# A causal attention kernel: the scores of the fifth row tile split as 256 and 384 keys instead of 512 and 128

## The chip, the cores and the metric

The kernel runs on one core of a Trainium2 chip, in one launch. The metric is the device time of that launch in microseconds (us); less is better. The core has five engines that run side by side and meet at semaphores: TensorE (PE in the profile; its weight loads are shown apart as PEld), VectorE (DVE), ScalarE (ACT), GpSimd (POOL) and SyncE (SP), which issues the loads and stores here.

## The reference

It is a layer norm followed by attention and a feed-forward part, both added to the input. What matters for the change is the attention, causal, with 16 heads of 128 columns over 2 batches of 1024 rows:

```python
q = (x @ Wq + bq).reshape(b, h, t, dh)
k = (x @ Wk + bk).reshape(b, t, h, dh).transpose(0, 2, 3, 1)
v = (x @ Wv + bv).reshape(b, t, h, dh).transpose(0, 2, 1, 3)
logits = jnp.einsum('bhtd,bhds->bhts', q, k) * scale
mask = jnp.triu(jnp.full((t, t), -jnp.inf, dtype=x.dtype), k=1)
weights = jax.nn.softmax(logits + mask, axis=-1)
out = jnp.einsum('bhts,bhsd->bhtd', weights, v)
```

All of it is float32. The input has 2048 rows of 256 columns, so there are 32 pairs of batch and head; they are called heads 0 to 31 here.

## The kernel before, in words

**Split products.** Each float32 operand is held as a high and a low part, and every product is three matmuls (`split_matmul`, lines 39 to 43): high by high (L41), high by low (L42), low by high (L43). So each operand that TensorE makes must come out of PSUM twice: ScalarE writes the high part, VectorE then subtracts it and writes the low part.

**Stages.** The norm, the first Q projections and the feed-forward part take the time up to about 324 us. Then come 256 steps, 8 for each head, one for each row tile of 128 rows (`for s in range(NH * TILES)`). Tile i needs the scores of (i + 1) * 128 keys. In a step TensorE transposes the probabilities of three steps ago (L1117), makes the scores of the present tile into one of two pairs of PSUM banks, and does a piece of other work: a projection of K or V, an output product, or a product of probabilities with V. The scores go to VectorE (mask and maximum, L921), to ScalarE (exponential, L480), to GpSimd (reciprocal and scaling, L696 and L699), and come back as transposes. The transposed blocks leave PSUM by ScalarE (`pt_hi`, L466) and VectorE (`pt_lo`, L832).

**Jobs and their one bank.** Projections of K and V and output products are called jobs. The tables `EVEN` and `ODD` put them into the steps, as FIRST (ahead of the scores), EARLY (behind them) or LATE. Nearly all share one PSUM bank, `M`. Before a job starts, TensorE waits (`run`, `freed_by`) until the low part of the job before it in that bank has been written by VectorE, as that is its last reader. In step 1 of a head the job K1 makes the right half of that head's keys (512 of them); the next job in `M` comes behind the scores of step 2, and is the output product O0a in even heads and the V projection V3 in odd ones. Some heads differ: heads 0 and 1 have no job in step 2, and in heads 7, 15 and 23 (`new_group`) steps 1, 2, 4 and 5 also hold Q projections of the next group. The K1 of head 31 is run in step 5 of head 30, with the output product O1a behind it in step 6.

**K buffers.** The left half of K lies in `k_even` or `k_odd`, by the head's number, each 512 columns wide; the right half in `k_right`. The fifth tile (i = QT = 4) needs 640 keys, and its scores are two groups of three matmuls: 512 keys of the left buffer into the first bank, 128 keys of the right buffer into the second.

**What sets the order.** Each engine's order is written out in the program; none is planned at run time. On ScalarE and VectorE a FIRST job is taken out of PSUM in step 1 ahead of what the step goes on with: on VectorE the masked maximum and the `pt_lo` of the next step stand behind it.

Of the kernel before, what the change touches and what calls it, by code (L numbers as in the profile page):

```python
# [12 lines left out]
F32, F32R = mybir.dt.float32, mybir.dt.float32r  # L13
BF16, I32, F8 = mybir.dt.bfloat16, mybir.dt.int32, mybir.dt.float8e4
ACT = mybir.ActivationFunctionType
ALU = mybir.AluOpType
AX = mybir.AxisListType

P = 128
BATCH, SEQ, DM = 2, 1024, 256  # L20
TOK = BATCH * SEQ
HEADS, DH = 16, 128
# [4 lines left out]
N = 512  # L27
# [7 lines left out]
def flat(ap):  # L35
    return ap.rearrange("p a b -> p (a b)")


def split_matmul(nc, out, w_hi, w_lo, m_hi, m_lo, start, stop):

    nc.tensor.matmul(out, w_hi, m_hi, start=start, stop=False)  # L41
    nc.tensor.matmul(out, w_hi, m_lo, start=False, stop=False)  # L42
    return nc.tensor.matmul(out, w_lo, m_hi, start=False, stop=stop)  # L43
# [12 lines left out]
def attention(nc, sh, d, out):  # L56
# [7 lines left out]
    QT = N // P  # L64
# [10 lines left out]
    S = [ps[:, 0:2, :], ps[:, 2:4, :]]  # L75
# [5 lines left out]
    with ExitStack() as c:  # L81
        sb = lambda name, shape, dt: c.enter_context(nc.sbuf_tensor(name, shape, dt))
        sem = lambda name: c.enter_context(nc.semaphore(name))
        minus_one = sh["minus_one"]
        mask_row = sb("mask_row", [P, SEQ], BF16)
        bq, bk, bv, wq_in, kv_in, kv_hi, kv_lo = (
            sh[name] for name in ("bq", "bk", "bv", "wq_in", "kv_in", "kv_hi", "kv_lo"))
# [4 lines left out]
        wq_hi, wq_lo = sb("wq_hi", [P, LOADS, KC, DH], F32R), sb("wq_lo", [P, LOADS, KC, DH], F32R)  # L92
        q_all = sb("q_all", [P, GROUP, SEQ // HEADS, HEADS], F32)
        q_hi, q_lo = sb("q_hi", [P, 2, N], F32R), sb("q_lo", [P, 2, N], F32R)
        k_even = [sb(name, [P, N], F32R) for name in ("k_hi_even", "k_lo_even")]
        neg_max, row_sum, inv_sum = (sb(name, [P, 2 * TILES], F32) for name in ("neg_max", "row_sum", "inv_sum"))


# [12 lines left out]
            minus_half, var_eps, rstd = (eb(name, [P, NT], F32) for name in ("minus_half", "var_eps", "rstd"))  # L111
        pt_hi, pt_lo = (sb(name, [P, 42, P], F32R) for name in ("pt_hi", "pt_lo"))
        o_hi, o_lo = sb("o_hi", [P, N], F32R), sb("o_lo", [P, N], F32R)
        k_odd = [sb(name, [P, N], F32R) for name in ("k_hi_odd", "k_lo_odd")]
        k_right = [sb(name, [P, N], F32R) for name in ("k_hi_right", "k_lo_right")]
        probs_all = sb("probs", [P, 26 * P], F32)
        v_hi, v_lo = (sb(name, [P, 2, TILES, DH], F32R) for name in ("v_hi", "v_lo"))
# [60 lines left out]
        def job_of(h, i, where):  # L178

            name = JOBS[h].get(i, {}).get(where)  # L180
            if name is None:
                return None
            if name[0] == "K":
                return ("K", h if name == "K1" else h + 1, int(name[1]))
            if name[0] == "V":
                return ("V", h // 2, int(name[1]))
            return ("O", h - 1, int(name[1]), "ab".index(name[2]))
# [15 lines left out]
        probs = lambda s, i: probs_all[:, (0, 5, 11, 18)[i % 4] * P:((0, 5, 11, 18)[i % 4] + i + 1) * P]  # L203
# [4 lines left out]
        def k_of(h, half):  # L208

            if half and h + 1 == NH:  # L210
                return [t[:, 0:N] for t in wq_space]
            return [t[:] for t in (k_right if half else (k_even, k_odd)[h % 2])]

        def q_of(h, half):

# [26 lines left out]
        bank_of = lambda *turn: S[place[turn] % 2]  # L242
# [25 lines left out]
        bank_for = lambda job: elsewhere.get(job, M)  # L268
# [112 lines left out]
        def _(act):  # L381
# [56 lines left out]
            def evacuate(job):  # L438

                if job is None or job[0] == "O":  # L440
                    return
                act.wait_ge(job_done, nth[job])
                if job[0] == "K":
                    _, h, half = job
                    ins = nc.scalar.activation(k_of(h, half)[0], bank_for(job), ACT.Identity,
                                               bias=bk[:, h % HEADS:h % HEADS + 1])
                else:
                    ins = nc.scalar.activation(v_view(v_hi, job[2]), as_v(bank_for(job)), ACT.Copy)  # L448
                ins.then_inc(job_hi_done, 1)
# [90 lines left out]
            for s in range(NH * TILES):  # L540
                h, i = divmod(s, TILES)
# [173 lines left out]
        def _(dve):  # L715
# [64 lines left out]
            def evacuate(job):  # L780

                if job is None:
                    return
                if job[0] == "K":
                    _, h, half = job
                    dve.wait_ge(job_hi_done, nth_hi[job])
                    k_hi, k_lo = k_of(h, half)
                    ins = nc.vector.scalar_tensor_tensor(k_lo, bank_for(job), bk[:, h % HEADS:h % HEADS + 1],
                                                         k_hi.bitcast(F32), ALU.add, ALU.subtract)
                elif job[0] == "V":  # L790
                    dve.wait_ge(job_hi_done, nth_hi[job])
                    ins = nc.vector.tensor_tensor(v_view(v_lo, job[2]), as_v(bank_for(job)),  # L792
                                                  v_view(v_hi, job[2]).bitcast(F32), ALU.subtract)
                else:
                    _, h, half, ab = job
                    dve.wait_ge(job_done, nth[job])
                    g = h // HEADS * (SEQ // P // 2) + 2 * half + ab
                    sums = flat_acc[:, g * PAIR:(g + 1) * PAIR]
                    ins = nc.vector.tensor_tensor(sums, bank_for(job), sums, ALU.add)  # L799
                ins.then_inc(job_lo_done, 1)  # L800

            def wq_low(n):
                dve.wait_ge(wq_hi_done, n + 1)
                slot = n % LOADS
                nc.vector.tensor_tensor(  # L805
                    flat(wq_lo[:, slot, :, :]), flat(wq_in[:, slot, :, :]), flat(wq_hi[:, slot, :, :]).bitcast(F32),
                    ALU.subtract).then_inc(wq_lo_done, 1)
# [18 lines left out]
            def pt_low(s, ch):  # L826

                i = tile_at(s)
                at = chunk_no(s, ch)
                blocks = min(QT, i + 1 - ch * QT)  # L830
                dve.wait_ge(pt_hi_done, at + 1)
                nc.vector.tensor_tensor(  # L832
                    pt_blocks(pt_lo, i, ch), T[at % 2][:, 0:blocks * P].rearrange("p (a b) -> p a b", b=P),
                    pt_blocks(pt_hi, i, ch).bitcast(F32), ALU.subtract).then_inc(pt_lo_done, 1)
# [76 lines left out]
            for s in range(NH * TILES):  # L911
                h, i = divmod(s, TILES)
                if s:
                    evacuate(job_of(*divmod(s - 1, TILES), LATE))
                if s >= LAG:
                    for ch in range(banks_of(tile_at(s - LAG))):
                        pt_low(s - LAG, ch)
                evacuate(job_of(h, i, FIRST))
                dve.wait_ge(scores_done, s + 1)
                tile, width = tile_of(h, i), (tile_of(h, i) + 1) * P  # L920
                nc.vector.tensor_tensor_reduce(  # L921
                    probs(s, tile), flat(bank_of("S", h, tile))[:, 0:width], mask_row[:, SEQ - width:SEQ],
                    -1.0, -MASKED, ALU.add, ALU.min, neg_max[:, s % 16:s % 16 + 1]).then_inc(max_done, 1)
                evacuate(job_of(h, i, EARLY))
                if s == 1:
                    add_down(*halves_at(STEPS + 1))
                    add_down(*halves_at(STEPS + 2))
                for m in o_after(h, i):
                    o_low(h - 1, m)
                if i < 2 and new_group(h):  # L930
                    for n in (2 * i, 2 * i + 1):
                        wq_low((h + 1) // GROUP * HEADS + n)
                for u in q_steps(h, i):
                    q_step(h // GROUP + 1, u)
# [15 lines left out]
        def _(pe):  # L950
# [135 lines left out]
            def scores(s):  # L1086
                h, i = divmod(s, TILES)
                tile = tile_of(h, i)
                bank_free("S", h, tile)
                if i == 0:  # L1090
                    pe.wait_ge(job_lo_done, nth[("K", h, 0)])
                if tile == QT:
                    pe.wait_ge(job_lo_done, nth[("K", h, 1)])
                half, cols = tile // QT, slice(tile % QT * P, (tile % QT + 1) * P)
                if i == 0 or tile == QT:
                    pe.wait_ge(q_lo_done, 2 * h + half + 1)
                hi, lo = q_of(h, half)
                for bank in range(half + 1):
                    width = min(N, (tile + 1) * P - bank * N)
                    keys_hi, keys_lo = k_of(h, bank)  # L1100
                    last = split_matmul(nc, bank_of("S", h, tile)[:, bank, 0:width], hi[:, cols], lo[:, cols],
                                        keys_hi[:, 0:width], keys_lo[:, 0:width], True, True)
                last.then_inc(scores_done, 1)

# [60 lines left out]
            for k in range(STEPS):  # L1165
# [9 lines left out]
                if k == BO_ROW_AT:  # L1175
                    pe.wait_ge(bo_wide_done, KC)
                    pe.wait_ge(wt_lo_done, 2 + k // 4)
                    for h in range(KC):
                        last = nc.tensor.transpose(M[:, h * P:(h + 1) * P], bo_wide[:, h, :], ident[:])
# [5 lines left out]
            for s in range(NH * TILES):  # L1185
                h, i = divmod(s, TILES)
# [73 lines left out]
```

## Time and profile before

| | us |
|---|---|
| median of 3 runs | 1260.76 (1258.79 to 1262.61) |
| the profiled execution's own time | 1260.4 |
| its span, first to last instruction | 1258.6 |
| PE busy / PEld busy | 1225.3 / 1084.6 |
| DVE / ACT / POOL busy | 876.2 / 741.1 / 742.7 |

The mean granted TensorE clock is 0.992 of full. In the timeline an instruction has its start and duration. Matmuls are pipelined and overlap in it, so that what one costs is the distance from its start to the start of the next one, not its duration; a weight load (PEld) normally starts when the matmul ahead of the one that it serves starts. Short waits of TensorE are not marked in brackets: they are seen as a weight load that starts late.

### The profile page before, as it was taken

What the parts mean: (1) busy time and instruction counts of PE and PEld (TensorE: products, weight loads), DVE (VectorE), ACT (ScalarE), POOL (GpSimd) and SP (SyncE); (2) the same over time, 40 slices, a digit from 0 to 9 for tenths busy, and PEclk for the clock granted to TensorE, in tenths of its full rate; (3) what the DMA queues carried; (4) which work ended last, traced back from release to release, by engine and by line L of the source; (5) the groups of instructions that cost most, each with busy time, mean ns of one, the idle gap of its engine ahead of it and who ended that gap; (6) DMA issues with size and microseconds to landing.
All of it is one profiled execution on the core that took longest, in us unless ns stands there. A gap on an engine that the chain in (4) does not pass through costs nothing.

```text
span 1258.6 us, 20567 instructions
## 1 busy us (share of the span) xinstructions
PE 1225.3 (97%) x7556; PEld 1084.6 (86%) x7556; DVE 876.2 (70%) x1695; ACT 741.1 (59%) x1534; POOL 742.7 (59%) x784
## 2 busy tenths in 40 slices
PE   8999999999999999999999999999999999999997
PEld 7788888888889999779999888899899779899886
DVE  8877777776766676656777666667677666676664
ACT  4544444444676667556676665576667566666653
POOL 6445545553676667347676742676767337677753
PEclk9999999999999999999999999999999999999999
DMA  6100000000000000110000011010000200000001
GB/s 151 46 7 14 13 14 11 23 1 9 13 13 14 27 14 13 51 30 27 13 14 14 25 36 47 14 46 14 26 14 13 64 1 22 18 14 14 14 5 34
DMA packets 57331, 29.87 MB, mean 24 GB/s; under 512 B 16272, under 2 KB 57232, under 8 KB 57232
## 3 DMA queue, kind: packets, MB, share of 16 engines
q1 hardware_dynamic: 56016, 27.62, 7.9%
q8 instruction: 62, 1.02, 0.3%
q10 hardware_dynamic: 1216, 0.93, 0.2%
q14 instruction: 37, 0.30, 0.1%
HBM read 26.44 MB, written 2.10 MB: 23 GB/s over the span
## 4 chain that ended last, share of the span: by engine, by line
PE 88%; DVE 7%; ACT 3%; POOL 1%; issue 1%; DMA 0%; ACTq 0%; POOLq 0%
PE ps L41 26%; PE ps L43 26%; PE ps L42 26%; PE ps L1117 9%; ACT probs L480 1%; DVE pt_lo L832 1%; DVE xn_rows L736 1%; DVE probs L921 1%; PE ps L985 1%; DVE wq_lo L805 1%; DVE q_all L814 1%; POOL probs L699 1%; ACT pt_hi L466 1%; DVE stats L721 0%; ACT wq_hi L386 0%
## 5 line engine op out<-in xcount | busy, mean ns | idle before, releaser
L699 POOL TENSOR_TENSOR probs<-probs,inv_sum 128x128 f32<-128x128 f32 (+7 forms) x256 | 294.9, 1152 | 20.0
L696 POOL TENSOR_TENSOR inv_sum<-row_sum,minus_one 128x1 f32<-128x1 f32 x256 | 141.1, 551 | 258.2 <-ACT probs L480 257.1
L480 ACT ACTIVATE probs<-probs,neg_max 128x128 f32<-128x128 f32 (+7 forms) x256 | 198.8, 777 | 109.6 <-DVE neg_max L921 107.1
L466 ACT ACTIVATE pt_hi<-ps 128x512 fp32r<-128x512 f32 (+3 forms) x384 | 173.7, 488 | 92.1 <-PE ps L1117 89.1
L832 DVE TENSOR_TENSOR pt_lo<-ps,pt_hi 128x512 fp32r<-128x512 f32 (+3 forms) x384 | 200.8, 551 | 16.9 <-ACT pt_hi L466 16.7
L921 DVE CUSTOM_DVE_ANT_0 probs<-ps,mask_row 128x128 f32<-128x128 f32 (+7 forms) x256 | 192.0, 750 | 14.7 <-PE ps L43 8.2
L1117 PE MATMUL ps<-ident,probs 128*128 128x128 f32 x1152 | 169.6, 275 | 5.2 <-DVE pt_lo L832 3.9
L682 POOL TENSOR_TENSOR hid_lo<-act_buf,hid_hi 128x512 fp32r<-128x512 f32 x64 | 82.9, 1295 | 140.7 <-ACT hid_hi L420 140.7
L1117 PEld LDWEIGHTS ps<-ident,probs 128*128 128x128 f32 x1152 | 134.9, 142 | 18.7 <-issue 8.9
L42 PE MATMUL ps<-pt_lo,v_hi 128*128 128x512 f32 (+3 forms) x386 | 133.8, 347 | 0.0
L43 PE MATMUL ps<-pt_hi,v_lo 128*128 128x512 f32 (+3 forms) x386 | 133.5, 346 | 0.0
L41 PE MATMUL ps<-pt_hi,v_hi 128*128 128x512 f32 (+3 forms) x386 | 131.2, 340 | 0.0
L799 DVE TENSOR_TENSOR acc<-ps,acc 128x512 f32<-128x512 f32 x128 | 87.6, 685 | 58.9 <-PE ps L43 58.8
L589 POOL TENSOR_TENSOR q_lo<-q_all,q_hi 128x512 fp32r<-128x512 f32 x63 | 81.8, 1299 | 71.3 <-ACT q_hi L457 71.3
L515 ACT ACTIVATE act_buf<-ps 128x512 f32<-128x512 f32 x64 | 38.3, 599 | 132.7 <-PE ps L43 132.7
L840 DVE SCALAR_TENSOR_TENSOR o_lo<-ps,bv,o_hi 128x512 fp32r<-128x512 f32 x63 | 47.3, 751 | 81.0 <-ACT o_hi L473 81.0
L41 PE MATMUL ps<-xn_hi,w_hi 128*128 128x512 f32 x256 | 102.9, 402 | 0.7 <-DVE act_buf L891 0.5
L42 PE MATMUL ps<-xn_lo,w_hi 128*128 128x512 f32 x256 | 101.3, 396 | 0.0
L43 PE MATMUL ps<-xn_hi,w_lo 128*128 128x512 f32 x256 | 101.0, 395 | 0.0
L792 DVE TENSOR_TENSOR v_lo<-ps,v_hi 128x512 fp32r<-128x512 f32 x64 | 44.3, 692 | 59.4 <-ACT v_hi L448 59.4
L41 PEld LDWEIGHTS ps<-pt_hi,v_hi 128*128 128x128 f32 x386 | 73.5, 190 | 9.0
L42 PEld LDWEIGHTS ps<-pt_lo,v_hi 128*128 128x128 f32 x386 | 73.2, 190 | 9.0
(151 smaller groups left out, 3394.4 us busy)
## 6 DMA issues: line engine op xcount, KB each, us to landing
wq_in<-in_wq SPq DMA_DIRECT2D x63, 128.0 KB, 2.3
kv_in<-in_wk SPq DMA_DIRECT2D x16, 256.0 KB, 2.5
wo_in<-in_wo SPq DMA_DIRECT2D x32, 128.0 KB, 2.0
kv_in<-in_wv SPq DMA_DIRECT2D x32, 128.0 KB, 2.3
out<-acc SPq DMA_DIRECT2D x8, 256.0 KB, 2.4
acc<-in_x SPq DMA_DIRECT2D x2, 512.0 KB, 5.5
raw<-in_gate SPq DMA_DIRECT2D x16, 64.0 KB, 1.7
raw<-in_up SPq DMA_DIRECT2D x16, 64.0 KB, 2.1
```

What stands on the lines that cost most here:

```text
L41: nc.tensor.matmul(out, w_hi, m_hi, start=start, stop=False)
L42: nc.tensor.matmul(out, w_hi, m_lo, start=False, stop=False)
L43: return nc.tensor.matmul(out, w_lo, m_hi, start=False, stop=stop)
L466: nc.scalar.activation(pt_blocks(pt_hi, i, ch), T[at % 2][:, 0:blocks * P].rearrange("p (a b) -> p a b", b=P), ACT.Copy).then_inc(pt_hi_do ...
L480: nc.scalar.activation(row, row, ACT.Exp, bias=neg_max[:, s % 16:s % 16 + 1], scale=-1.0, accum_out=row_sum[:, s % 16:s % 16 + 1]).then_in ...
L682: nc.gpsimd.tensor_tensor(hid_lo[:, k % 4, :], act_buf[:, k % 4, :], hid_hi[:, k % 4, :].bitcast(F32), ALU.subtract).then_inc(hid_lo_done, 1)
L696: nc.gpsimd.tensor_tensor(inv_sum[:, at], row_sum[:, at], minus_one[:], ALU.pow).then_inc(inv_done, 1)
L699: nc.gpsimd.tensor_tensor(row, row, inv_sum[:, at].to_broadcast([P, (tile_of(h, i) + 1) * P]), ALU.mult).then_inc(probs_done, 1)
L799: ins = nc.vector.tensor_tensor(sums, bank_for(job), sums, ALU.add)
L832: nc.vector.tensor_tensor(pt_blocks(pt_lo, i, ch), T[at % 2][:, 0:blocks * P].rearrange("p (a b) -> p a b", b=P), pt_blocks(pt_hi, i, ch). ...
L921: nc.vector.tensor_tensor_reduce(probs(s, tile), flat(bank_of("S", h, tile))[:, 0:width], mask_row[:, SEQ - width:SEQ], -1.0, -MASKED, ALU ...
L1117: last = nc.tensor.transpose(T[at % 2][:, n * P:(n + 1) * P], probs(s, i)[:, b * P:(b + 1) * P], ident[:])
```

## The change

The left K buffers become 640 columns wide. When the right half of K leaves PSUM, its first 128 keys are also written into the new fifth block of the left buffer, by an extra instruction on ScalarE and one on VectorE, each ahead of the one that writes the 512 columns. The fifth tile's scores are then 256 keys and 384 keys, all from the left buffer. They lie in columns 256 to 895 of the two banks, next to one another as before, and VectorE reads them from there.

```diff
-        k_even = [sb(name, [P, N], F32R) for name in ("k_hi_even", "k_lo_even")]
+        k_even = [sb(name, [P, N + P], F32R) for name in ("k_hi_even", "k_lo_even")]
-        k_odd = [sb(name, [P, N], F32R) for name in ("k_hi_odd", "k_lo_odd")]
+        k_odd = [sb(name, [P, N + P], F32R) for name in ("k_hi_odd", "k_lo_odd")]
...
+        k_fifth = lambda h: [t[:, N:N + P] for t in (k_even, k_odd)[h % 2]]
+        k_middle = lambda h: [t[:, 2 * P:N + P] for t in (k_even, k_odd)[h % 2]]
+        score_cols = lambda tile: slice(2 * P, 2 * P + N + P) if tile == QT else slice(0, (tile + 1) * P)
...
                 act.wait_ge(job_done, nth[job])
                 if job[0] == "K":
                     _, h, half = job
+                    if half:
+                        nc.scalar.activation(k_fifth(h)[0], bank_for(job)[:, 0:P], ACT.Identity,
+                                             bias=bk[:, h % HEADS:h % HEADS + 1])
                     ins = nc.scalar.activation(k_of(h, half)[0], bank_for(job), ACT.Identity,
                                                bias=bk[:, h % HEADS:h % HEADS + 1])
...
                     dve.wait_ge(job_hi_done, nth_hi[job])
+                    if half:
+                        k_hi, k_lo = k_fifth(h)
+                        nc.vector.scalar_tensor_tensor(k_lo, bank_for(job)[:, 0:P], bk[:, h % HEADS:h % HEADS + 1],
+                                                       k_hi.bitcast(F32), ALU.add, ALU.subtract)
                     k_hi, k_lo = k_of(h, half)
                     ins = nc.vector.scalar_tensor_tensor(k_lo, bank_for(job), bk[:, h % HEADS:h % HEADS + 1],
                                                          k_hi.bitcast(F32), ALU.add, ALU.subtract)
...
-                    probs(s, tile), flat(bank_of("S", h, tile))[:, 0:width], mask_row[:, SEQ - width:SEQ],
+                    probs(s, tile), flat(bank_of("S", h, tile))[:, score_cols(tile)], mask_row[:, SEQ - width:SEQ],
...
-                    width = min(N, (tile + 1) * P - bank * N)
+                    first, width = 0, min(N, (tile + 1) * P - bank * N)
                     keys_hi, keys_lo = k_of(h, bank)
-                    last = split_matmul(nc, bank_of("S", h, tile)[:, bank, 0:width], hi[:, cols], lo[:, cols],
+                    if tile == QT and bank == 0:
+                        first, width = 2 * P, 2 * P
+                    elif tile == QT:
+                        width = 3 * P
+                        keys_hi, keys_lo = k_middle(h)
+                    last = split_matmul(nc, bank_of("S", h, tile)[:, bank, first:first + width], hi[:, cols], lo[:, cols],
```

On VectorE, step 1 and the start of step 2 and 3 of an even head read before as follows (`k_lo_right` is the low part of the right half, L921 the masked maximum of scores, `acc` takes up the output product O0a):

```order
L832 TENSOR_TENSOR pt_lo<-ps,pt_hi 128x3x128 [waits pt_hi_done]
L788 SCALAR_TENSOR_TENSOR k_lo_right<-ps,bk,k_hi_right 128x512 [waits job_hi_done]
L921 ISA probs,neg_max<-ps,mask_row 128x256 [waits scores_done]
L921 ISA neg_max 128x1
L832 TENSOR_TENSOR pt_lo<-ps,pt_hi 128x4x128 [waits pt_hi_done] x2
L921 ISA probs,neg_max<-ps,mask_row 128x384 [waits scores_done]
L921 ISA neg_max 128x1
L799 TENSOR_TENSOR acc<-ps,acc 128x512 [waits job_done]
```

The same place now, in the changed kernel's line numbers:

```order
L843 TENSOR_TENSOR pt_lo<-ps,pt_hi 128x3x128 [waits pt_hi_done]
L796 SCALAR_TENSOR_TENSOR k_lo_even<-ps,bk,k_hi_even 128x128 [waits job_hi_done]
L799 SCALAR_TENSOR_TENSOR k_lo_right<-ps,bk,k_hi_right 128x512
L932 ISA probs,neg_max<-ps,mask_row 128x256 [waits scores_done]
L932 ISA neg_max 128x1
L843 TENSOR_TENSOR pt_lo<-ps,pt_hi 128x4x128 [waits pt_hi_done] x2
L932 ISA probs,neg_max<-ps,mask_row 128x384 [waits scores_done]
L932 ISA neg_max 128x1
L810 TENSOR_TENSOR acc<-ps,acc 128x512 [waits job_done]
```

One instruction of 128 columns is new, and the wait for ScalarE's high parts moved to it; all else of the step stands behind both. ScalarE has the like: the 128-column write (L450) first, with the wait for the job, then the 512-column one (L452).

On TensorE, the fifth tile of an even head read before (`k_hi_even` is the left buffer, `k_hi_right` the right one, `vw_hi` the start of the V projection behind it):

```order
L1117 MATMUL ps<-ident,probs 128x128
L41 MATMUL ps<-k_hi_even,q_hi 128x512 [waits q_lo_done,job_lo_done,max_done]
L42 MATMUL ps<-k_lo_even,q_hi 128x512
L43 MATMUL ps<-k_hi_even,q_lo 128x512
L41 MATMUL ps<-k_hi_right,q_hi 128x128
L42 MATMUL ps<-k_lo_right,q_hi 128x128
L43 MATMUL ps<-k_hi_right,q_lo 128x128
L41 MATMUL ps<-vw_hi,xn_hi 128x256 [waits vw_lo_done,job_lo_done]
```

And now:

```order
L1133 MATMUL ps<-ident,probs 128x128
L41 MATMUL ps<-k_hi_even,q_hi 128x256 [waits q_lo_done,job_lo_done,max_done]
L42 MATMUL ps<-k_lo_even,q_hi 128x256
L43 MATMUL ps<-k_hi_even,q_lo 128x256
L41 MATMUL ps<-k_hi_even,q_hi 128x384
L42 MATMUL ps<-k_lo_even,q_hi 128x384
L43 MATMUL ps<-k_hi_even,q_lo 128x384
L41 MATMUL ps<-vw_hi,xn_hi 128x256 [waits vw_lo_done,job_lo_done]
```

The count of matmuls and the sum of their columns stay; only the widths and the buffer of the second three differ.

## Rows read from the trace of the kernel before

**Rows 1.** The page, chain that ended last, share of the span by engine
```profile
PE 88%; DVE 7%; ACT 3%; POOL 1%; issue 1%; DMA 0%; ACTq 0%; POOLq 0%
```

**Rows 2.** Timeline of PE, fifth tile of head 14: start, duration, instruction
```profile
721.10 0.48 PE L41 MATMUL ps<-k_hi_even,q_hi 128*128 128x512 f32 x1
...
722.16 0.33 PE L41 MATMUL ps<-vw_hi,xn_hi 128*128 128x256 f32 x1
722.33 0.28 PE L42 MATMUL ps<-vw_lo,xn_hi 128*128 128x256 f32 x1
```

**Rows 3.** Timeline of PE: widths 256 behind transposes, and 384
```profile
702.75 0.37 PE L41 MATMUL ps<-wo_hi,o_hi 128*128 128x256 f32 x1
...
703.19 0.28 PE L41 MATMUL ps<-wo_hi,o_hi 128*128 128x256 f32 x1
...
703.53 0.39 PE L41 MATMUL ps<-k_hi_odd,q_hi 128*128 128x512 f32 x1
...
704.22 0.34 PE L41 MATMUL ps<-k_hi_right,q_hi 128*128 128x384 f32 x1
...
704.74 0.27 PE L1117 MATMUL ps<-ident,probs 128*128 128x128 f32 x1
```

**Rows 4.** Timeline of head 14, steps 1 to 3: VectorE
```profile
714.83 0.75 DVE L788 SCALAR_TENSOR_TENSOR k_lo_right<-ps,bk,k_hi_right 128x512 fp32r<-128x512 f32 x1 [0.36 <-ACT k_hi_right L445]
...
715.49 0.41 DVE L921 CUSTOM_DVE_ANT_0 probs<-ps,mask_row 128x256 f32<-128x256 f32 x1
```

**Rows 5.** The same stretch: TensorE, its weight loads
```profile
715.63 0.19 PEld L41 LDWEIGHTS ps<-wo_hi,o_hi 128*128 128x128 f32 x1
...
716.63 0.14 PEld L1117 LDWEIGHTS ps<-ident,probs 128*128 128x128 f32 x1 [0.24 <-issue]
```

**Rows 6.** The same stretch: TensorE, its matmuls
```profile
715.65 0.36 PE L41 MATMUL ps<-wo_hi,o_hi 128*128 128x256 f32 x1
...
715.85 0.28 PE L42 MATMUL ps<-wo_lo,o_hi 128*128 128x256 f32 x1
```

**Rows 7.** Timeline of head 2, first with a job in step 2: VectorE and weight load
```profile
375.51 0.75 DVE L788 SCALAR_TENSOR_TENSOR k_lo_right<-ps,bk,k_hi_right 128x512 fp32r<-128x512 f32 x1 [0.36 <-ACT k_hi_right L445]
...
376.32 0.19 PEld L41 LDWEIGHTS ps<-wo_hi,o_hi 128*128 128x128 f32 x1
```

**Rows 8.** Timeline of head 30, step 5, the last K1: ScalarE, VectorE, weight load
```profile
1204.16 0.69 ACT L445 ACTIVATE wq_hi<-ps,bk 128x512 fp32r<-128x512 f32 x1 [2.10 <-PE ps L43]
1204.74 0.62 ACT L457 ACTIVATE q_hi<-q_all 128x512 fp32r<-128x512 f32 x1
1204.88 0.75 DVE L788 SCALAR_TENSOR_TENSOR wq_lo<-ps,bk,wq_hi 128x512 fp32r<-128x512 f32 x1 [1.14 <-ACT wq_hi L445]
1205.69 0.19 PEld L41 LDWEIGHTS ps<-wo_hi,o_hi 128*128 128x128 f32 x1 [0.23 <-DVE wq_lo L788]
```

**Rows 9.** Groups by form, ScalarE from 320 us: count, busy us, mean ns
```profile
L466 ACT ACTIVATE pt_hi<-ps 128x128 fp32r<-128x128 f32 x64 | 17.1, 267 | 3.0 <-PE ps L1117 3.0
L473 ACT ACTIVATE k_hi_right<-ps,bv 128x256 fp32r<-128x256 f32 x2 | 0.9, 475 | 0.9 <-PE ps L43 0.9
```

**Rows 10.** Groups by form, VectorE from 320 us
```profile
L832 DVE TENSOR_TENSOR pt_lo<-ps,pt_hi 128x128 fp32r<-128x128 f32 x64 | 18.1, 283 | 3.6 <-ACT pt_hi L466 3.6
L840 DVE SCALAR_TENSOR_TENSOR k_lo_right<-ps,bv,k_hi_right 128x256 fp32r<-128x256 f32 x2 | 1.0, 484 | 0.6 <-ACT k_hi_right L473 0.6
```

**Rows 11.** Timeline of TensorE: waits in head 1 and head 7, steps 1 to 3
```profile
352.16 0.30 PE L1117 MATMUL ps<-ident,probs 128*128 128x128 f32 x1 [0.83 <-DVE pt_lo L832]
...
508.76 0.47 PE L41 MATMUL ps<-xn_hi,wq_hi 128*128 128x512 f32 x1 [1.85 <-DVE wq_lo L805]
```

**Rows 12.** Windows: length, busy (count) of five engines, granted PE clock
```profile
506.00:512.00 6.00, 4.15 (x20) 3.06 (x20) 4.63 (x10) 2.97 (x8) 1.42 (x2) 1.00 0.31 89
551.70:555.10 3.40, 3.38 (x10) 2.82 (x11) 0.30 (x2) 0.49 (x2) 3.19 (x4) 0.50 0.00 0
744.00:750.00 6.00, 5.03 (x18) 4.08 (x19) 3.50 (x6) 2.87 (x7) 1.42 (x2) 0.72 0.33 90
```

More of the change, by code:

```diff
@@ L211, in k_of @@
                 return [t[:, 0:N] for t in wq_space]
-            return [t[:] for t in (k_right if half else (k_even, k_odd)[h % 2])]
+            return [t[:, 0:N] for t in (k_right if half else (k_even, k_odd)[h % 2])]
+        k_fifth = lambda h: [t[:, N:N + P] for t in (k_even, k_odd)[h % 2]]
+        k_middle = lambda h: [t[:, 2 * P:N + P] for t in (k_even, k_odd)[h % 2]]
+        score_cols = lambda tile: slice(2 * P, 2 * P + N + P) if tile == QT else slice(0, (tile + 1) * P)
         def q_of(h, half):
```

## The prediction

> **What bounds the kernel now.** I read the chain of waits first: 88% of it is TensorE [rows 1]. So what a change saves or adds on TensorE's path counts in full, and work on another engine counts only where TensorE comes to wait for it. Then TensorE's timeline in the fifth tile, for what the two widths cost; then the timeline of all engines in steps 1 to 3 of a head, because the change puts new instructions there. What the reader is to see in the second is how the weight load of the job in step 2 stands to VectorE's `k_lo_right`, which is the last reader of the one PSUM bank that the job needs.
>
> **The change, first part: narrower and wider matmuls in the fifth tile.** In head 14 the first score matmul starts at 721.10 and the second matmul of the next job at 722.33, so 1.23 us [rows 2]. I count up to that second matmul on purpose. The 128-column matmuls are fed by weight loads that come about 0.11 us apart, each later than its matmul could have used it, and the first matmul behind them pays the rest: it takes 0.17 us (722.16 to 722.33) [rows 2], where plain 256-column ones take (703.53 - 703.19) / 3 = 0.113 us [rows 3]. The tile as it will be is composed of rows of the same shapes: three of 256 columns behind transposes, 702.75 to 703.19, 0.44 us; three of 384 columns, 704.22 to 704.74, 0.52 us; then one plain 256-column matmul of the next job, 0.115 us [rows 3]. The sum is 1.075 us. The gain is 1.23 - 1.075 = 0.155 us for a head, on TensorE's path. With 32 heads, 5.0 us. If the late start behind the 128s were not given back, it would be 0.10 us for a head, 3.2 us; nothing in the rows makes it more than 0.155 us. Nothing waits in that place, so I take 5.0 us.
>
> **Second part: 128 more columns on ScalarE and on VectorE.** Neither instruction is in the trace, so each is bounded by neighbours. On ScalarE the same function with a bias takes 0.475 us at 256 columns [rows 9] and 0.69 us at 512 [rows 8]. The slope is 0.215 us for 256 columns, so 128 columns would take 0.475 - 0.107 = 0.368 us. Instructions of one engine overlap: the 0.69 us one at 1204.16 is followed at 1204.74, 0.58 us later [rows 8], so 0.10 us is taken off: 0.265 us. On VectorE the same operation takes 0.484 us at 256 columns [rows 10] and 0.75 us at 512, and is followed after 0.66 us (714.83 to 715.49) [rows 4]. That makes 0.484 - 0.133 - 0.085 = 0.266 us. The nearest 128-column rows, of simpler operations, are 0.267 us on ScalarE [rows 9] and 0.283 us on VectorE [rows 10] in duration. Less the same overlaps they give the lower ends, 0.17 and 0.20 us; the upper ends are the full durations of the biased forms, 0.37 and 0.35 us. VectorE's first read waits until ScalarE has written both high parts, so the two add up: the low part of K's right half is done 0.265 + 0.266 = 0.53 us later (0.37 to 0.72).
>
> By the Trainium skill ("ScalarE: Activation LUTs", section What ACT_TABLE_LOAD costs) such an instruction with a pointer bias takes about 280 ns + 0.833 ns a column, and back-to-back ones overlap by about 93 ns. That is 0.29 us instead of 0.265 for the new one, and would make the sum below 0.8 us larger. For 512 columns it says 0.71 us, where the row has 0.69.
>
> **Who waits for it.** The job behind the scores of step 2 may not start before `k_lo_right` is done. In head 14 that ends at 714.83 + 0.75 = 715.58, and the job's first weight load starts at 715.63 [rows 4, 5]. The job's first matmul takes 0.20 us (715.65 to 715.85) [rows 6] instead of 0.113. So TensorE already waits there, by nearly 0.09 us, too short to be shown in brackets: there is no slack. It is the same in every head that has this job: 375.51 + 0.75 = 376.26 and 376.32 in head 2, the first [rows 7]; 1204.88 + 0.75 = 1205.63 and 1205.69 for the K1 of head 31, the last [rows 8]. Between them lie the other heads with a job in step 2, even and odd alike, all but 7, 15 and 23: 27 places in all. There the whole 0.53 us falls on TensorE.
>
> Behind the waiting job, TensorE has the transposes of step 3. In even heads they too wait for VectorE, for the `pt_lo` behind `k_lo_right` and the maximum: the weight load is late by 0.24 us at 716.63 [rows 5]. That `pt_lo` moves by the same 0.53 us, as it is queued behind the two instructions, so this wait stays as long as it was and gives nothing back. Later steps are released by scores and transposes that TensorE itself makes 0.53 us later, so ScalarE, VectorE and GpSimd move with it.
>
> Head 1 has no job in step 2, but its step 3 waits 0.83 us for the same `pt_lo` [rows 11], and so pays the full 0.53 us. In heads 7, 15 and 23 TensorE waits 1.85 us in step 1 for a `wq_lo` of VectorE [rows 11], whose high part stands on ScalarE behind the exponential, and that behind VectorE's maximum. VectorE is late there with other work, so ScalarE's extra is hidden and only VectorE's 0.27 us goes through: 3 x 0.27 = 0.8 us. In head 0 the K1 is taken out behind the maximum and the additions after it wait for matmuls: I take nothing, at most 0.5 us. No DMA and no SP or GpSimd instruction is moved, and the mask and maximum of the fifth tile read as many columns as before: nothing.
>
> **The sum.** 28 x 0.53 = 14.9 us, plus 0.8, less 5.0: 10.7 us slower. The profiled execution took 1260.4 us with a span of 1258.6, so it would take 1271.1; against the median of 1260.76 that is 1271.5 us. With the ends for the two instructions: 28 x 0.37 + 3 x 0.20 - 5.0 = 6.0 us, and 28 x 0.72 + 3 x 0.35 - 3.2 = 18 us.
>
> **The rivals.**
>
> *The bank is not what TensorE waits for: faster.* If the weight load at 715.63 is late for another reason, say the change from one operand's buffer to another, and `k_lo_right` has slack of over 0.53 us, then only the first part counts: 1260.8 - 5.0 = 1255.8 us. For it: no wait is put down to `k_lo_right` in head 14. Against it: 0.05 us from VectorE's end to the load in the first, the middle and the last of 27 places, with different steps around them, and the bracket in the last names VectorE [rows 4, 5, 7, 8]. It decides from the point where the 0.53 us exceed the slack; I see a slack of zero. 5%.
>
> *Waits further on give part of it back.* If the wait in step 3 of the 15 even heads from 2 to 30 shrinks as TensorE arrives later, 15 x 0.24 = 3.6 us come back: 7.1 us slower, 1267.9 us. For it: that wait exists [rows 5]. Against it: its releaser stands behind the new instructions in VectorE's order. 10%.
>
> *The clock.* In the 3.4 us from 551.70 TensorE is granted 0.50, the lower of its levels of 1.2 and 2.4 GHz, behind a wait for GpSimd's `q_lo`. Around the wait in step 1 of head 15 the mean is 0.72 over 6 us, which is one such stretch, and around that of head 7 it is 1.00 [rows 12]. These waits become 0.27 us longer. If the two heads that kept the full clock (7 and 23) fall too, that is 2 x 3.4 x 0.5 = 3.4 us more: 1274.9 us. It can as well go the other way by 1.7 us, if head 15 keeps it. 12%. The Trainium skill ("TensorE: Matmul & The Clock Gate", Part 1: The HAM clock gate) has this as a rule: an idle TensorE falls back to 1.2 GHz, and where the fall comes depends also on the phase of a free-running window; that two like waits differ in the trace agrees with it.
>
> *The small instructions cost their full durations.* Then the delay is 0.72 us: 28 x 0.72 + 3 x 0.35 - 5.0 = 16.2 us, 1277.0 us. Against it: every pair back to back in the rows overlaps. 8%.
>
> That the change does not do what it says I leave out: the order of the instructions has both widths and both new instructions.
>
> **How the numbers follow.** The forecast has 65%, at 1271.5 us. The range is 1265.5 to 1277.5: it takes in the bounds of the two small instructions nearly in full, the rival of waits given back and the clock; it leaves out the faster case and the far end. A change within 0.3% (3.8 us) could not be told from none. Only a mixture of small delay, waits given back and a better clock ends there: 4%. Faster by more has the 5% of the first rival, slower 91%.
>
> **What would show it.** In the profile after: (1) `k_hi_even<-ps,bk` and `k_lo_even<-ps,bk,k_hi_even` (and the odd ones) at 128 columns, some 0.37 and 0.35 us long, 32 of each. (2) `k_lo_right` starts 0.53 us later behind the end of K1's matmuls than now, and the job's weight load still starts 0.05 us behind its end. Now TensorE's wait is some 0.6 us and shown in brackets, with VectorE's `k_lo_right` as what ended it, in 27 places. (3) The fifth tile takes 1.075 us up to the second matmul of the next job. (4) The wait in step 3 of even heads is still 0.24 us. I am wrong if the job's weight load comes earlier than `k_lo_right` ends, if the extra delay is under 0.37 us, or if TensorE's other waits shrink.

## The result and the profile after

| | before | after |
|---|---|---|
| median of 6 runs, us | 1260.06 (1258.72 to 1262.61) | 1270.08 (1267.77 to 1272.88) |
| profiled execution, span, us | 1260.4, 1258.6 | 1270.97, 1269.2 |
| mean granted TensorE clock | 0.992 | 0.992 |

The changed kernel is slower: the ratio is 1.008, with a 95% interval of 1.0063 to 1.0096, so 10.0 us at the medians. 1271.5 was forecast. One execution of the kernel before, among the repeats beside the last experiments, took 6423 us in the slow state, and no difference below counts it.

The page's chain of waits has moved, against [rows 1], from TensorE to the two engines that got the new instructions:

```profile
PE 84%; DVE 9%; ACT 5%; POOL 1%; issue 1%; DMA 0%; ACTq 0%; POOLq 0%
```

The place is best seen in the chain itself, here steps 1 and 2 of head 14 in the changed kernel (start, us, what):

```profile
719.88 0.25 PE ps L43
720.12 0.02 issue
720.15 0.37 ACT k_hi_even L450
720.52 0.59 ACT k_hi_right L452
721.11 0.03 issue
721.13 0.35 DVE k_lo_even L796
721.48 0.67 DVE k_lo_right L799
722.15 0.04 issue
722.19 0.38 PE ps L41
```

From the end of K1 to the start of the next job in its bank, the path leaves TensorE and runs through all four instructions that empty the bank. Two of them are new (L450, L796). The timeline of the same stretch has the starts of the VectorE pair and of the weight load, which answer to [rows 4, 5]:

```profile
721.13 0.35 DVE L796 SCALAR_TENSOR_TENSOR k_lo_even<-ps,bk,k_hi_even 128x128 fp32r<-128x128 f32 x1 [0.62 <-ACT k_hi_right L452]
...
721.40 0.74 DVE L799 SCALAR_TENSOR_TENSOR k_lo_right<-ps,bk,k_hi_right 128x512 fp32r<-128x512 f32 x1
...
722.19 0.19 PEld L41 LDWEIGHTS ps<-wo_hi,o_hi 128*128 128x128 f32 x1 [0.65 <-DVE k_lo_right L799]
```

`k_lo_right` ends at 721.40 + 0.74 = 722.14 and the weight load follows 0.05 us later, as before; only now it is 0.65 us late, and the bracket names its releaser. The question who waited for line 799 gives the count:

```profile
who waited for it (us, times):
  PEld ps L41: 17.5, 27
```

The fifth tile, to be held against [rows 2]:

```profile
727.65 0.36 PE L41 MATMUL ps<-k_hi_even,q_hi 128*128 128x256 f32 x1
...
728.09 0.34 PE L41 MATMUL ps<-k_hi_even,q_hi 128*128 128x384 f32 x1
...
728.61 0.28 PE L41 MATMUL ps<-vw_hi,xn_hi 128*128 128x256 f32 x1
728.73 0.28 PE L42 MATMUL ps<-vw_lo,xn_hi 128*128 128x256 f32 x1
```

727.65 to 728.73 is 1.08 us, where it was 1.23; the first matmul behind it takes 0.12 us instead of 0.17.

### The profile page after: what moved, and what is told of

The parts are those of the page before. It is cut to its first block, busy times and chain, and to the rows that moved or that the text cites. A ratio compares the mean times of both kernels' runs of the same rounds, so it can differ in the third digit from the quotient of the medians.

```text
span 1269.2 us, 20631 instructions
## 1 busy us (share of the span) xinstructions
PE 1226.0 (97%) x7556; PEld 1084.2 (85%) x7556; DVE 883.9 (70%) x1727; ACT 747.6 (59%) x1566; POOL 742.3 (58%) x784
## 4 chain that ended last, share of the span: by engine, by line
PE 84%; DVE 9%; ACT 5%; POOL 1%; issue 1%; DMA 0%; ACTq 0%; POOLq 0%
PE ps L41 26%; PE ps L43 25%; PE ps L42 25%; PE ps L1133 7%; DVE k_lo_right L799 2%; ACT k_hi_right L452 1%; DVE xn_rows L743 1%; DVE pt_lo L843 1%; ACT probs L487 1%; DVE probs L932 1%; PE ps L996 1%; DVE wq_lo L816 1%; DVE q_all L825 1%; POOL probs L706 1%; ACT pt_hi L473 0%
## 5 line engine op out<-in xcount | busy, mean ns | idle before, releaser
L41 PE MATMUL ps<-wo_hi,o_hi 128*128 128x256 f32 x252 | 78.1, 310 | 5.8 <-DVE k_lo_right L799 4.9
```

## The experiments

Medians and ratios are against the kernel before on the same chip. The "two heads" are from the last matmul of K1 in head 12 to that in head 14, in the timeline; it is a measure without the stages ahead and behind and without stretches of low clock.

| run | median, us | ratio (95%) | two heads, us |
|---|---|---|---|
| before | 1258.9 to 1260.1 | | 713.67 - 662.09 = 51.58 |
| changed kernel | 1270.08 | 1.008 (1.0063 to 1.0096) | 719.72 - 667.38 = 52.34 |
| new instructions alone | 1275.96 | 1.0134 (1.0118 to 1.0149) | 720.33 - 667.75 = 52.58 |
| new widths alone | 1254.48 | 0.9967 (0.9955 to 0.998) | 711.87 - 660.61 = 51.26 |
| ScalarE's alone | 1268.72 | 1.0077 (1.0064 to 1.0089) | 717.04 - 664.94 = 52.10 |
| VectorE's alone | 1268.75 | 1.0081 (1.0067 to 1.0094) | 718.49 - 666.48 = 52.01 |
| copies on GpSimd | 1256.29 | 0.9978 (0.9968 to 0.9989) | 712.38 - 661.07 = 51.31 |
| copies behind, own engines | 1260.86 | 1.0011 (1.0003 to 1.002) | 713.94 - 662.37 = 51.57 |
| changed kernel, K1 in step 0 | 1307.46 | 1.0382 (1.0368 to 1.0396) | |
| before, K1 in step 0 | 1294.17 | 1.0276 (1.0262 to 1.029) | |
| GpSimd's copies, K1 in step 0 | 1289.95 | 1.0246 (1.0232 to 1.026) | |

**The two halves apart.** The first run adds only the new instructions, the second only the widths:

```diff
 # new instructions alone: both blocks "if half: ... k_fifth(h) ..." on ScalarE and VectorE;
 # scores and maximum as in the kernel before
 # new widths alone:
-                    if half:
+                    if half and h < 2:
```

> The two new 128-column instructions alone; the scores of the fifth tile stay 512 and 128 keys. My theory: the job behind the scores of step 2 starts 0.51 to 0.53 us later in 27 places and head 1 waits as much longer, so all of the change's loss and none of its gain: 10.0 + 5.0 = 15 us slower than before, 1275 us; in the profile the same wait of 0.6 us for k_lo_right as in the changed kernel. If the gain of the widths is only 0.10 us for a head: 13.2 us slower. If instead the new widths or the columns they lie in cause the loss: no change, 1260 us. If the clock makes a part of it: fewer than 28 x 0.5 us on the waits and more stretches at half clock.

> The scores of the fifth tile as 256 and 384 keys, but the fifth block is written in heads 0 and 1 only; all later heads read those stale keys, so their fifth tile's scores are not the reference's. My theory: 5.0 us faster than before less 0.5 us for the block written in head 1, 1255.6 us, and the tile takes 1.08 us up to the second matmul of the next job instead of 1.23. Rival, the late start behind 128-column matmuls is not given back: 3.2 - 0.5 = 2.7 us faster, 1257.4 us. Rival, the time is taken up again by a later wait: 1260 us.

The instructions alone cost 17.1 us and the widths alone bring 4.4 us. In two heads that is +1.00 and -0.32 us, together 0.68, where the changed kernel has +0.76; the medians give 17.1 - 4.4 = 12.7 where it has 10.0, so the parts add up to within some 3 us. The loss is wholly the new instructions', and the gain is there in full: 0.16 us a head. The run with the widths alone reads stale keys in 30 heads, so its results are wrong; it shows what the widths are worth in time. The waits in the run with the instructions alone have this row (idle time in us in total, times, the longest). It has 26 of the 27 places; the last one, in head 30, stands under the name `wq_lo`:

```profile
PEld ps L41 <- DVE k_lo_right L797: 16.7, 26, 0.6
```

17.1 us is 2.1 more than was expected, and the instructions are not the reason. The profiled executions have spans of 1274.1 and 1258.6 us, so 15.5 us between them, where 15 was expected. What is lower is the kernel before in the repeats of this experiment, with a median of 1258.9 us, where its profiled execution took 1260.4.

**One engine at a time.**

```diff
 # ScalarE's alone (kernel before with)
+                    if half:
+                        nc.scalar.activation(k_fifth(h)[0], bank_for(job)[:, 0:P], ACT.Identity, bias=...)
 # VectorE's alone (kernel before with)
+                    if half:
+                        k_hi, k_lo = k_of(h, 1)[0][:, 0:P], k_fifth(h)[1]
+                        nc.vector.scalar_tensor_tensor(k_lo, bank_for(job)[:, 0:P], bk[...], k_hi.bitcast(F32), ...)
```

> The kernel before with ScalarE's new 128-column instruction alone, VectorE's left out; scores as before. My theory: TensorE's wait grows by ScalarE's 0.265 us in 28 places and not in heads 7, 15 and 23: 7.4 us slower, 1267.5 us. If the loss came from VectorE being the busier engine: under 2 us. If waits were given back in step 3 of even heads: 3.4 to 4 us slower.

> The kernel before with VectorE's new 128-column instruction alone (it subtracts the first 128 columns of the right buffer's high part), ScalarE's left out; scores as before. My theory: 0.26 us more in 28 places and in heads 7, 15 and 23: 28 x 0.26 + 3 x 0.26 = 8.1 us slower, 1268.1 us; with the run of ScalarE alone it adds up to the run with both. If the two new instructions overlapped each other, the single runs would add up to more than the run with both.

Each alone makes the wait, in the same places and of the same size. The first row is ScalarE's run, the second VectorE's:

```profile
PEld ps L41 <- DVE k_lo_right L793: 10.0, 26, 0.4
```

```profile
PEld ps L41 <- DVE k_lo_right L794: 10.0, 26, 0.4
```

From K1's last matmul to the second one of the waiting job, the median over heads is 2.18 us before, 2.44 with either instruction, and 2.70 with both: 0.26 + 0.26 = 0.52. They add up and do not overlap. ScalarE has much idle time (busy 741 of 1259 us before), and its 0.26 us costs as much there as VectorE's: what counts is the row of four instructions, not how busy the engine is. In heads 7, 15 and 23 the prediction had another answer, that ScalarE's instruction is hidden and only VectorE's comes through. It is so. The row of that wait is 5.6 us in three times before; again the first row is ScalarE's run, the second VectorE's:

```profile
PE ps L41 <- DVE wq_lo L810: 5.6, 3, 1.9
```

```profile
PE ps L41 <- DVE wq_lo L811: 6.3, 3, 2.1
```

The timed medians (9.8 and 9.9 us) are above the 7.4 and 8.1 expected; the spans of the profiled executions differ from that before by 8.5 and 7.5 us.

That the two add up is also a matter of the order chosen: `k_lo_even` waits for both of ScalarE's writes, and VectorE is idle for 0.62 us ahead of it (the bracket at 721.13). A `k_lo_even` that waited for the 128-column write alone would have room there, and the delay could be some 0.26 instead of 0.52 us. That is an estimate from this row; no run has tried it.

**Releasing the bank first.** The same new widths in heads 0 to 30, but the fifth block is copied out of the right buffer by GpSimd, which stands idle at that point:

```diff
+                if i == 1 and h + 1 < NH:
+                    pool.wait_ge(job_lo_done, nth[("K", h, 1)])
+                    for to, of in zip(k_fifth(h), k_right):
+                        nc.gpsimd.tensor_copy(to, of[:, 0:P]).then_inc(fifth_done, 1)
```

> The fifth tile's widths of the changed kernel in heads 0 to 30, but the fifth block is not taken out of PSUM: in step 1 GpSimd copies it, high and low, from the right buffer, once that is done, and the fifth tile waits for it. ScalarE and VectorE are as before the change. My theory: the bank is free as early as before, GpSimd is idle in that place for over a microsecond, so the gain of the run with stale keys without its loss in head 1, 31 x 0.155 = 4.8 us faster than before: 1254.1 us. Rival, the copies delay GpSimd's reciprocal of the step and by it the transposes three steps on: 1258 us or more. Rival, GpSimd's traffic slows VectorE: over 1258 us too.

2.8 us faster than before, clear of noise (the interval ends at 0.9989), and so about 13 us faster than the changed kernel. This is the version that beats both. In its timeline, head 14, the copies take GpSimd about 0.5 us and it is idle again ahead of the reciprocal:

```profile
714.35 0.29 POOL L703 CAST k_hi_even<-k_hi_right 128x128 fp32r<-128x128 f32 x1 [0.61 <-DVE k_lo_right L797]
714.58 0.29 POOL L703 CAST k_lo_even<-k_lo_right 128x128 fp32r<-128x128 f32 x1
715.34 0.55 POOL L705 TENSOR_TENSOR inv_sum<-row_sum,minus_one 128x1 f32<-128x1 f32 x1 [0.46 <-ACT probs L485]
```

Both rivals (a late reciprocal, a slower VectorE) fall with that and with the two heads, 51.31 us, 0.27 less than before. Over 31 heads that is 4.2 us; the medians have 2.8 of them, the spans of the profiled executions (1254.6 and 1258.6) 4.0.

The other way to release the bank first leaves the work on ScalarE and VectorE:

```diff
                 ins.then_inc(job_lo_done, 1)
+                if job[0] == "K" and job[2] and job[1] + 1 < NH:
+                    dve.wait_ge(job_lo_done, nth[job])
+                    nc.vector.tensor_copy(k_fifth(job[1])[1], k_right[1][:, 0:P].bitcast(F32)).then_inc(fifth_done, 1)
 # and the like on ScalarE behind job_hi_done
```

> As the run with GpSimd's copies, but ScalarE and VectorE make the copies of the fifth block themselves, out of the right buffer, each right behind its 512-column instruction; so they have as many new instructions as in the changed kernel, but the bank is released ahead of them. My theory: the weight load of the job in step 2 comes as early as before the change (2.18 us from K1's last matmul to the job's second, against 2.70 in the changed kernel), so the odd heads lose nothing. VectorE's maximum and pt_lo still come 0.3 to 0.35 us later, so the wait in step 3 of the 15 even heads grows from 0.24 to about 0.6 us, and heads 1, 7, 15 and 23 lose as much: 19 x 0.33 = 6.3 us lost, 4.8 won, 1.5 us slower than before, 1260.7 us. If it were the work on the two engines that costs, and not the release of the bank: as the changed kernel, 10 us slower. If the wait in step 3 gave its part back: 4 us faster.

1.6 us slower, where 1.5 was expected; the interval, 1.0003 to 1.002, only just leaves out no change. The two engines have one new instruction each a head, as in the changed kernel (in 31 heads instead of 32), and the loss of 10 us is down to 1.6. The copies are somewhat shorter than the instructions that they replace, 0.31 and 0.23 us against 0.37 and 0.35, so this run does not hold the work quite equal; but the wait for the bank is back to 2.18 us although the work is there. What is left of the loss is in step 3 of even heads, head 14:

```profile
715.88 0.23 DVE L811 CAST k_lo_even<-k_lo_right 128x128 fp32r<-128x128 f32 x1
...
715.90 0.19 PEld L41 LDWEIGHTS ps<-wo_hi,o_hi 128*128 128x128 f32 x1
...
717.16 0.14 PEld L1135 LDWEIGHTS ps<-ident,probs 128*128 128x128 f32 x1 [0.50 <-issue]
717.20 0.30 PE L1135 MATMUL ps<-ident,probs 128*128 128x128 f32 x1 [0.32 <-DVE pt_lo L843]
```

The job's weight load starts at 715.90 while the copy has only just begun, so it does not wait for it; but the transposes behind wait 0.50 us for `pt_lo`, where [rows 5] have 0.24. That is the second wait of the prediction, seen by itself.

**A miss: K1 earlier.** If the bank is emptied too late, start K1 earlier:

```diff
-        EVEN = {0: {EARLY: "K0"}, 1: {FIRST: "K1"}, ...
+        EVEN = {0: {EARLY: "K0", LATE: "K1"}, ...
-        ODD = {0: {EARLY: "V2"}, 1: {FIRST: "K1"}, ...
+        ODD = {0: {EARLY: "V2", LATE: "K1"}, ...
```

> The changed kernel with the job K1 at the end of step 0 instead of ahead of the scores of step 1 (heads 1 to 30). My theory: the distance from K1 to the next job in its bank grows by the seven transposes between, 0.7 us, which is more than the wait of 0.6 us that the change made, so the 27 waits go. But K1 then comes 0.7 us earlier behind the job before it in the bank, whose low part was done at 711.95 in head 14, where K1 would want to start at 711.7: a new wait of about 0.3 us. Net 27 x 0.3 = 8 us faster than the changed kernel, 1261 us. If the wait for the bank were not the cause of the loss: no faster than the changed kernel, 1269 us or more.

> The kernel before with K1 at the end of step 0 and nothing else. My theory: the short waits of 0.09 us in 27 places and 0.24 us in 15 go, a wait of about 0.3 us ahead of K1 comes in up to 29 places: 1 to 3 us slower than before, 1261 us. If that new wait does not come, 6 us faster: 1253 us.

> The copy on GpSimd together with K1 at the end of step 0. My theory: the sum of the two, 1256 us, so no better than the copy alone. If K1's place costs nothing: 1248 us.

All three came out 34 to 38 us slower than their counterparts, where 8 us faster, 1 to 3 us slower and about no difference were expected. In the waits of the kernel before with K1 in step 0 the cause stands in one row; the second row is the same one without the move:

```profile
PE ps L1117 <- DVE pt_lo L832: 34.0, 31, 1.9
```

```profile
PE ps L1117 <- DVE pt_lo L832: 3.9, 5, 1.9
```

That is 30 of the 35 us. In the changed kernel with K1 in step 0, where VectorE has one instruction more in that place, the row has 48.4 us in 32 times. The new wait of 0.3 us ahead of K1 that I had expected is there too, but in 12 places only, 3.1 us in all.

I had counted the bank and not VectorE's order. K1's low part is now taken out ahead of the `pt_lo` of the step. K1's bank is free at 704.54 + 0.75 = 705.29, early enough, but the `pt_lo` can start only then, at 705.21 in the overlap of the two, and TensorE's next transposes stand still until 706.01, as they wait for it:

```profile
704.54 0.75 DVE L788 SCALAR_TENSOR_TENSOR k_lo_right<-ps,bk,k_hi_right 128x512 fp32r<-128x512 f32 x1 [0.83 <-ACT k_hi_right L445]
705.21 1.15 DVE L832 TENSOR_TENSOR pt_lo<-ps,pt_hi 128x512 fp32r<-128x512 f32 x2
706.01 0.86 PEld L1117 LDWEIGHTS ps<-ident,probs 128*128 128x128 f32 x8 [1.31 <-issue]
706.04 1.06 PE L1117 MATMUL ps<-ident,probs 128*128 128x128 f32 x8 [1.14 <-DVE pt_lo L832]
```

The waits for `k_lo_right` are gone here, so that part of the mechanism was right, and the move is useless all the same: a job moved on TensorE takes its emptying with it on two other engines.

## Why the prediction was right

**The widths, 5.0 us.** The changed tile takes 1.08 us where 1.075 was composed. Counting up to the second matmul of the next job was what made it 0.155 us and not 0.10: the run with the widths alone has 0.16 us a head. Its median moved by 4.4 us, with 4.5 expected (5.0 less the 0.5 us for the block written in head 1).

**The two instructions.** L450 and L796 take 0.37 and 0.35 us, and the next starts 0.26 and 0.27 us behind each, against 0.265 and 0.266 taken. The extrapolation from 512 and 256 columns of the same form held within hundredths; the 128-column rows of simpler forms [rows 9, 10] would have been 0.10 us (ScalarE) and 0.07 us (VectorE) too short in duration. The distance of 0.26 us on ScalarE is that of the rows and not the 0.29 us named beside it.

**Who waits.** 27 places, the count forecast, and 0.52 us each instead of 0.53. Head 1 pays in full, as forecast: its wait in step 3 goes from 0.83 [rows 11] to 1.36 us. Heads 7, 15 and 23 pay VectorE's part alone: the wait for `wq_lo` goes from 5.6 to 6.4 us over the three, 0.27 us each. The load follows 0.05 us behind `k_lo_right` in head 14 as before. The rival that the bank is not waited for falls with the waits' row and with the run on GpSimd. That waits further on give part back falls too: in step 3 of head 14 the load is late by 0.25 us after, where it was 0.24 [rows 5].

```profile
723.20 0.14 PEld L1133 LDWEIGHTS ps<-ident,probs 128*128 128x128 f32 x1 [0.25 <-issue]
```

**The sum.** With the measured sizes 28 x 0.52 + 3 x 0.26 - 32 x 0.155 = 10.4 us; the spans of the two profiled executions differ by 10.6 us and the medians by 10.0. That the spans come within 0.1 us of the 10.7 forecast has some luck in it: both executions happen to have the same number of stretches at half clock, six, and one more or less would have moved the difference by 1.6 us.

**The clock.** In the profiled executions each kernel has one of the three heads with a wait in step 1 at low clock, but not the same one: head 15 before [rows 12], head 7 after. These are the windows around the waits of heads 7, 15 and 23 in the changed kernel:

```profile
508.80:514.80 6.00, 3.88 (x11) 2.77 (x10) 3.90 (x10) 2.77 (x7) 1.42 (x2) 0.72 0.26 73
747.00:753.00 6.00, 3.87 (x17) 2.79 (x17) 5.03 (x11) 3.16 (x8) 1.93 (x3) 1.00 0.20 56
988.00:994.00 6.00, 3.87 (x20) 2.88 (x19) 4.46 (x10) 3.13 (x8) 1.42 (x2) 1.00 0.25 69
```

So the longer waits did not make more stretches at half clock in this pair, and the rival did not come. With the other runs there are eight executions to look at. Where the wait for `wq_lo` has its old length of 1.9 us, the stretch comes in head 15 (before), in head 23 (widths alone and ScalarE's alone) and in none (copies on GpSimd). Where it is 2.1 us long, it comes in head 7 (changed kernel), in head 23 (instructions alone), in heads 7 and 23 (VectorE's alone) and in head 15 (copies behind). That is 3 of 12 against 5 of 12, too few to say whether the longer wait makes a fall more likely. A stretch in one of these heads costs 1.56 us: from K1's last matmul to the second one of the next job it is 11.36 us in head 15 before and 9.80 us in heads 7 and 23. The prediction had taken 1.7.

The clock explains a part of what the timed medians are off, by 1.8 to 2.4 us in three runs and by 1.4 us in the run on GpSimd, against its 4.2. Among the runs of one kernel, 0.001 less of the mean granted clock goes with 0.7 us more (an estimate: one slope through the recorded executions of each kernel, without the one of 6423 us). Brought to the same clock, 0.992, the differences of the means are 16.0 us for the instructions alone, 8.2 for ScalarE's, 8.7 for VectorE's and -4.0 for the run on GpSimd, where 15, 7.4, 8.1 and -4.8 were expected. In ScalarE's profiled execution there are eight stretches instead of six. One comes early on, in a window where the kernel before has a clock of 1.00, and one near the end, where it has 0.93:

```profile
27.00:33.00 6.00, 5.56 (x22) 4.56 (x23) 6.00 (x7) 0.94 (x1) 6.00 (x6) 0.72 0.42 76
1208.00:1232.00 24.00, 21.02 (x123) 18.72 (x122) 13.69 (x27) 12.63 (x26) 10.95 (x10) 0.86 0.00 1
```

The early one costs next to nothing, as TensorE is not what the kernel waits for there: K1's last matmul in head 0 starts at 326.73, and at 326.60 in the run with both instructions and no such stretch. No run takes the clock alone away, so that it makes these differences is likely and not shown, and it leaves up to 1 us of them open.

## What to carry to other kernels

Where a bank or buffer is handed on through a row of engines, the time until its release is the sum of that row, whatever share of the time each engine is idle. Look for it as a weight load that starts a few hundredths behind the end of the last reader, again and again at the same distance: a wait too short for the profile to mark has no slack, and everything added ahead of the release is paid in full. Release first and make further copies afterwards, from the buffer already written, and on an engine that is idle at that point.

When a step is moved for the sake of one wait, follow its instructions on every engine's order. And a saving from wider matmuls is to be counted to a point where the weight loads have caught up, not to the last matmul changed.

## What the hardware showed that was not expected

TensorE's low-clock stretches stand at different places in the profiled executions, also where the waits are nearly alike. The kernel before waits 1.85, 1.86 and 1.89 us in heads 7, 15 and 23, and the granted clock falls in the second alone; the changed kernel waits 2.12, 2.13 and 2.13 us, and it falls in the first alone. The executions of one kernel differ by 1 to 5 us; the clock goes with a part of that, and no profile here tells the rest apart.
